# A gather loop on GpSimd: the clear behind each indirect transfer comes behind every second one

## What is computed

```python
h = relu(layernorm(x))
x = x + L0(h, edge_weight, edge_attr_3)     # per edge: (relu(w*w1+b1) @ w2 + b2) and the edge's direction
                                            # mix the features of its source; summed per destination
h = relu(layernorm(x))
h = relu(conv(h, W1, b1))                   # conv: h @ W, rows taken by src, times norm, summed by dst
h = relu(conv(h, W2, b2))
x = x + relu(conv(h, W3, b3))
```

## Time and profile before

| | |
|---|---|
| median of three runs | 5770.3 us |
| span of the profiled execution, first to last instruction | 5779.7 us |
| the profiled execution's own time | not among the times shown |
| mean granted TensorE clock | 0.816 of full speed |
| busy: PE, DVE, ACT, POOL | 4258.6, 3608.0, 2702.7, 4889.1 us |
| indirect transfers on GpSimd | 3616 |
| clears of `pause` on GpSimd | 3616 |

### The profile page before, as it was taken

How to read it: one execution, slowest core, us unless ns; L and a number is a source line. 1 busy time by engine, 2 the same in 40 slices (tenths; PEclk the granted TensorE clock), 3 DMA queues, 4 the chain that set the end, 5 groups by cost and what they waited for, 6 DMA issues and landing times.

```text
span 5779.7 us, 179150 instructions
## 1 busy us (share of the span) xinstructions
PE 4258.6 (74%) x62463; PEld 3147.7 (54%) x62464; DVE 3608.0 (62%) x8469; ACT 2702.7 (47%) x6550; POOL 4889.1 (85%) x7276
## 2 busy tenths in 40 slices
PE   5777777777777777755555555889898889766666
PEld 3444444444444444444444444778787778554554
DVE  8777777777777777776666666333333334555555
ACT  4444444444444444466666666344444444433333
POOL 7888888888888888768888888688888889588886
PEclk9999999999999999955555555899989999767767
DMA  3111111111111111333332332332333333444444
GB/s 87 33 33 33 33 33 31 33 33 33 33 33 32 32 33 33 36 71 77 77 77 77 77 77 71 114 90 85 91 91 85 91 91 100 119 119 126 122 127 107
DMA packets 494970, 400.88 MB, mean 69 GB/s; under 512 B 269575, under 2 KB 454828, under 8 KB 493537
## 3 DMA queue, kind: packets, MB, share of 16 engines
q10 hardware_dynamic: 146996, 207.67, 10.6%
q0 software_dynamic: 115712, 109.02, 10.3%
q1 hardware_dynamic: 231536, 74.48, 5.9%
HBM read 375.52 MB, written 15.29 MB: 68 GB/s over the span
## 4 chain that ended last, share of the span: by engine, by line
POOL 50%; issue 40%; PE 5%; POOLq 2%; DVE 2%; DMA 1%; ACT 0%; DVEq 0%; SPq 0%
POOL rows L782 29%; POOL pause L762 21%; POOLq L761 2%; PE radial L2067 2%; PE psX L2082 1%; PE psT L2082 1%; PE sums L2153 1%; PE radial L2209 0%; DMA table<-arena 0%; PE radial L2222 0%; DMA rows<-table,idx 0%; DMA xn<-in_x 0%; POOLq L760 0%; PE radial L2008 0%; DVE rows L1827 0%
## 5 line engine op out<-in xcount | busy, mean ns | idle before, releaser
L782 POOL DMA_INDIRECT rows<-table,idx x3616 | 3636.6, 1006 | 803.0 <-POOL pause L762 483.7
L762 POOL MEMSET pause<- 128x256 f32 x3616 | 1234.8, 341 | 2.5
L1942 PEld LDWEIGHTS sums<-scratch,onehot 128*64 128x64 f32 x9408 | 789.7, 144 | 465.0 <-DVE scratch L1377 228.6
L2067 PE MATMUL radial<-arena,shared 128*32 128x96 bf16 (+1 forms) x31200 | 926.4, 266 | 154.2 <-DVE shared L1613 75.1
L1942 PE MATMUL sums<-scratch,onehot 128*64 128x264 f32 (+1 forms) x9408 | 984.1, 356 | 32.6 <-DVE scratch L1377 26.2
L2067 PEld LDWEIGHTS radial<-arena,shared 128*32 128x32 bf16 (+1 forms) x31200 | 664.8, 116 | 294.4 <-issue 72.0
L2153 PE MATMUL sums<-onehot,rows 128*128 128x80 f32 (+1 forms) x2844 | 371.0, 298 | 576.7 <-DMA rows<-table,idx 571.8
L1007 ACT CAST scratch<-radial 128x480 bf16<-128x480 f32 x860 | 476.9, 555 | 665.7 <-PE radial L2067 657.6
L1360 DVE TENSOR_TENSOR scratch<-radial,shared 128x768 f32<-128x768 f32 x784 | 743.4, 948 | 0.0
L1927 PE MATMUL radial<-shared 64*128 64x384 f32 x3136 | 730.5, 546 | 0.0
L880 ACT COPY shared<-rows 128x192 f32<-128x192 f32 x196 | 89.4, 456 | 1264.1 <-DMA rows<-table,idx 1262.9
(11 more groups left out here) (237 smaller groups left out, 5969.3 us busy)
## 6 DMA issues: line engine op xcount, KB each, us to landing
scratch<-places_d ACTq DMA_DIRECT2D x242, 800.0 KB
rows<-table,idx POOLq DMA_INDIRECT x3616
shared<-in_edge_weight SPq DMA_DIRECT2D x390, 128.0 KB, 2.9
idx<-in_src SPq DMA_DIRECT2D x451, 4.0 KB
table<-arena SPq DMA_DIRECT2D x24, 256.0 KB, 2.8
table<-arena SPq DMA_DIRECT2D x2, 1176.0 KB, 10.6
accT<-in_edge_attr SPq DMA_DIRECT2D x2, 1152.0 KB
table<-arena SPq DMA_DIRECT2D x24, 96.0 KB, 2.0
```

Source lines behind the costliest of these rows:

```text
L762: nc.gpsimd.memset(pause[:, :], 0.0).then_inc(made, 1)
L782: (pool.indirect_dma_start(rows_3[:, r, j, :] if n in (1, 3) else rows[:, r, j, 0:WIDTH[n]], None, tables[n], bass.IndirectOffsetOnAxis(ap ...
L1942: last = nc.tensor.matmul(there, onehot[:, u % 2, 4 * h + t, 0:SW], taken_from, start=(h + q + part == 0), stop=(h == 1 and q == 1 and par ...
L2067: last = nc.tensor.matmul(d, from_src[n][:, h, i, t, :], table_of(n, s), start=True, stop=True, tile_position=(0, 32 * i))
```

## The change

GpSimd now runs `pause_between` only behind the transfers with odd j: four clears in a group of eight transfers instead of eight. The counts that the waits compare with are halved to match, in the peeled steps and in the register.

```diff
                 if step.peeled:
-                    before = TPG * (sum(GATHERED[:n]) + step.it * step.groups + u) + j
+                    before = (TPG * (sum(GATHERED[:n]) + step.it * step.groups + u) + j) // 2
                     if before:
                         pool.wait_ge(made, 9 + before)
...
                                  .then_inc(gathered[r], 16))
-                            pause_between(step, n, u, j)
+                            if j % 2 == 1:
+                                pause_between(step, n, u, j)
...
-                pool.reg_mov(pauses, 9 + TPG * (sum(GATHERED[:n]) + LOOP[n][0]))
+                pool.reg_mov(pauses, 9 + TPG // 2 * (sum(GATHERED[:n]) + LOOP[n][0]))
                 sweep(pool, body, n)
```

## The result

The changed kernel takes 5343.4 us (four runs, 5339.2 to 5344.2) against 5769.2 us for the kernel before in the same rounds: a ratio of 0.926, 95% interval 0.925 to 0.927. That is 426 us less. The forecast was 550 less, 5220 us, with a range of 5080 to 6200.

The account below looks back on a forecast made before the run. GpSimd was taken to bound the kernel; dropped clears at 0.327 us gave 251, 120, 95 (capped by TensorE) and 84 us in layers 0 to 3, together 550 us off 5770.3, so 5220 us, range 5080 to 6200.

Parts of the forecast that it names:

- The bound: Gather loops of all layers: GpSimd's transfers, clears and gaps set the pace, over 90% of the chain that ended last.
- the price of a dropped clear: GpSimd in the gather loops: each dropped clear saves its 0.327 us, the 0.16 us gap staying ahead of every transfer.
- rival "slower": Second transfer of each pair, all layers: itself longer, a loss from 1.28 us; 5900 to 6180 us; chance 0.40.
- far end: Upper end for a lengthened transfer behind a transfer: 2.39 us, seen among the first 32; some 0.10 lies towards it.
- Layer 2's cap: Layer 2: TensorE becomes the bound, so 95 us are booked of its 110.9 us wait for gathered rows, not 131.
- The gap didn't close: Rival, gap ahead of each second transfer: it vanishes, another 0.161 us each, 240 us in all, 4980 us; chance 0.08.
- VectorE's hold-up: Rival, layer 0: transfers hold up VectorE's two-input instructions, 1.1 us each, cancelling the gain; about 5765 us; chance 0.05.
- The 101 us of long transfers: Layer 0: transfers' time over 0.953 us each, tied to VectorE's work and kept unchanged at 101 us.
- The index loads and the DMA engines: Loads come earlier by themselves; DMA engines rise from 0.17 to 0.42 to 0.19 to 0.47 of their time; nothing charged.

Follow-up runs that it names:

- the one it can't be told from: The changed kernel with clears of one column (128x1) behind every second transfer; 4916.8 us, 0.851 of the kernel before.

## Why the prediction was right in direction and a fifth off in size

**The bound.** Right: GpSimd alone set the pace in the gather loops, and time taken off its path came off the kernel. The forecast was 550 us; it was 426.

**The step that failed** is the price of a dropped clear, "its 0.327 us on the path", and in it "The gap of 0.16 us stands ahead of the transfer, not of the clear: I keep it". Behind a transfer the gap is 0.305 us. 0.144 us of each clear had been running in time that passes anyway, so that, with the 0.009 us by which the next transfer is shorter, the term was 0.192 us: 147 instead of 251 us in layer 0, 71 instead of 120 in layer 1, 49 instead of 84 in layer 3. The argument for it, "a clear behind a transfer starts with no gap at all, so nothing of the transfer hangs over its record", read an absence: a clear could start there and a transfer couldn't. The rival "slower" had the right suspicion, that the clear covers work of the transfer; its size stayed under the 0.33 us that decide the sign. (Its far end was misread: the longest transfer before took 2.62 us, among the first 32, not 2.39.)

**What came on top.** Each loop lost more than its share of 0.192. In layer 0, 188 - 147 = 41 us. Some 17 of it are shorter transfers: the group of POOL there went from 1558.3 us to 1533.8, and 7 of these 24 us are in the 0.192 already. Another 22 are waits that the profile gives no cause for, a term that the prediction put at nothing. Before, there were 30.0 us in 47 such waits. Thirty-one of them are ordinary gaps of 0.16 us; the other sixteen stand ahead of the 18th of 32 transfers in every third turn of layer 0's hardware loop, fifteen of them some 1.62 us long, as here in the kernel before:

```profile
364.83 1.17 POOL L782 DMA_INDIRECT rows<-table,idx  x1 [1.62 <-issue]
```

After, all 796 waits of this kind in layer 0 are the 0.30 us ones:

```profile
POOL rows L782 <- issue: 238.1, 796, 0.3
```

Over the four loops the kernel before has 45 long gaps, 22, 21, 17 and 7 us over an ordinary gap; the changed kernel has none. The kernels with a short clear behind each transfer have them, those with a clear behind every second or none do not (but for waits for row buffers late in layer 2). The sequencer's records tell more. Ahead of fifteen of the sixteen transfers in layer 0, 2.9 us pass between its wait (L761) and its next move (L760), against 0.54 elsewhere. After, at the same transfers, it is 3.5 against 0.99: the sequencer still stops for some 2.4 us, but it is further ahead. Before, it ran the waits of a group (L778) 1.0 to 1.5 us before the group's first transfer, with one transfer queued; now it is 2.4 to 2.7 us, with two, and GpSimd no longer notices the stop. What stops it no row tells.

In layer 2, beside 17 us of such gaps and 7 of shorter transfers, 16 us come from clears that took longer than 0.327: their mean there was 0.375 us, and all 144 clears over 0.4 us overlap VectorE's L1613.

With 0.192 us a clear, the prediction's sum would have been 344 us without a cap, 206 less than 550. The terms just told gave nearly half of that back; that the total is no more than about a fifth off is in part luck.

**Layer 2's cap** was right in sum by luck. I booked 95 us; the loop lost 116, and 20 came back between layers 2 and 3, where TensorE still had bucket work when the last transfer had ended: 96. But in the loop TensorE did not become the bound. GpSimd didn't wait for row buffers (0.2 us in all), and TensorE was busy 94%, not over 97; it still waited 48.9 us for gathered rows, where the forecast left 16 of the 110.9:

```profile
PE sums L2154 <- DMA rows<-table,idx: 48.9, 25, 4.8
```

So this wait gave 62 us and not 95. Most of the rest is a term that the prediction didn't have: the same matmuls took less time. The stretch of layer 2 and the one behind it, to layer 3, hold 19528 matmuls before and 19529 after, and these took 1192 and 1156 us, 36 less, while the granted clock in layer 2 went from 0.93 to 0.96. The stretches between layers 2 and 3, before and after:

```profile
4930.00:4998.00 68.00, 58.10 (x466) 28.71 (x464) 36.55 (x105) 42.52 (x105) 19.89 (x40) 0.85 0.49 146
...
4526.00:4614.00 88.00, 77.54 (x793) 45.40 (x792) 44.60 (x121) 49.90 (x126) 19.72 (x38) 0.88 0.39 114
```

**Rivals.** The gap didn't close, it opened. The prediction took from the Trainium skill ("GPSIMD Engine Reference", section "2.1 Instruction dispatch": a core goes on to the next instruction when its own share is done) that some cores might begin a transfer early. No row shows that: the spacing without clears, 1.249 us, is longer than record plus 0.16. VectorE's hold-up is real but tiny. The group of L1326 averaged 769 ns after against 758 before, and its wait for ScalarE fell from 535.5 to 343.4 us:

```profile
DVE shared L1327 <- ACT shared L888: 343.4, 186, 5.6
```

So of the rule in the Trainium skill, "SBUF — State Buffer", section "SBUF: two separate sides", that the first to start holds the port pair for its whole instruction, the runs bear out that one engine holds up the other; but a transfer held up VectorE only at its head (0.04 us in the row at 1011.16), not over its whole 0.95 us (L1557 in the earlier trace rows).

**The 101 us of long transfers** that I kept unchanged were not constant: what sets them is the spacing, and the change moved it. The index loads and the DMA engines cost nothing that a row shows. (The trace had lost no transfer, as the earlier trace rows show; the stretches of the earlier trace rows begin seven transfers into each loop.)

## What to carry to other kernels

On an in-order engine the cost of an instruction is the change in start-to-start time of its neighbours, not its record: what stands in the gap can be seen only with the instruction gone, and a one-column version of it comes close in spacing (1.252 against 1.249 us here), though not in time (77 us). A filler on the engine that sets the pace is worth a run without it at all; here 4922 us, or 0.852 of before, which beats both kernels of this case. When two engines hold each other up at fixed points, any change of rhythm moves the price; count the meetings before and after instead of carrying their cost over.

## What the runs showed of the hardware that was not expected

- An indirect transfer of 128 rows is followed by a fixed 0.305 us before the next one's record starts, in all four layers; a clear can run in the front 0.14 us of it. What GpSimd does in that time no row tells; it isn't the wait for the clear, nor a late sequencer. Nor did any run show a use of the clears: with none, the kernel was the fastest but for the one it can't be told from.
- A transfer waits at its start for a VectorE instruction with two inputs in SBUF and then ends 0.83 us after it (L1326 and L1338 in layer 0, 377 transfers before).
- GpSimd's sequencer stopped for some 2.4 us at fixed places of the loop, once in 96 transfers of layer 0. With one transfer queued ahead that left gaps of 1.62 us, with two it left none.
- TensorE's granted clock rose as gathers came closer: in layer 0 from 0.92 to 0.96 and 1.00 of full speed, in layer 2 from 0.93 to 0.96 and 0.99 (before, after, no clears). With the same matmuls its busy time fell from 1818 to 1745 and 1694 us in layer 0 (some 14,050 each), so at a higher clock the same work took less time. In layer 1 it stayed at 0.54 to 0.58, nearer to the 1.2 GHz level.
